# Filler products on TensorE through the routing of a two-choice expert tower

## What is computed

```python
h = embed_table[ids] @ proj_up.T                       # low-rank embedding, rank 64
h = h + attention(layernorm(h))                        # linear: no softmax, one sequence at a time
n = layernorm(h)
pg = softmax(n @ Wg + bg); gw, gi = top_k(pg, 2)       # 4 groups, two are taken
pe = softmax(n @ We + be); ew, ei = top_k(pe, 1)       # 4 experts in each group, one is taken
f(x) = gelu(x @ W1 + b1) @ W2 + b2                     # one expert, hidden size 768
out = sum of gw * ew * f_expert(n) over the two taken  # 16 experts in all
h = h + layernorm(out @ Wp + bp) * gamma + beta
```

## Time and profile before

| what | before |
|---|---|
| median of three runs | 295.75 us (295.14 to 296.15) |
| the profiled execution's own time | 294.89 us |
| its span | 293.1 us |
| mean granted clock of TensorE | 0.906 of full |
| TensorE matmul busy | 244.2 us (83%) |
| VectorE, ScalarE, GpSimd busy | 135.7, 113.3, 127.7 us |
| chain that ended last, by engine | PE 52%, DVE 16%, issue 15%, POOL 7%, ACT 5%, DMA 4% |

### The profile page before, as it was taken

How to read it: one execution, slowest core, us unless ns; L and a number is a source line. 1 busy time by engine, 2 the same in 40 slices (tenths; PEclk the granted TensorE clock), 3 DMA queues, 4 the chain that set the end, 5 groups by cost and what they waited for, 6 DMA issues and landing times.

```text
span 293.1 us, 8691 instructions
## 1 busy us (share of the span) xinstructions
PE 244.2 (83%) x3013; PEld 226.6 (77%) x3013; DVE 135.7 (46%) x498; ACT 113.3 (39%) x416; POOL 127.7 (44%) x142
## 2 busy tenths in 40 slices
PE   7899996210658999999999999999999999748960
PEld 7677774000558999999999999999999999747740
DVE  7616888879951324332233223322332332304795
ACT  4434557400002344244434433444344334408960
POOL 5773551447488445444544454445444441210000
PEclk9959999655577999999999999999999999969995
DMA  4410442060899995689729229595299220039022
GB/s 78 80 29 9 106 112 54 1 163 1 203 244 242 257 238 160 149 215 212 193 67 242 69 67 227 134 241 162 67 230 242 69 70 27 27 103 343 28 92 98
DMA packets 55034, 39.20 MB, mean 134 GB/s; under 512 B 30130, under 2 KB 52164, under 8 KB 55012
## 3 DMA queue, kind: packets, MB, share of 16 engines
q1 hardware_dynamic: 50004, 26.51, 38.1%
q0 software_dynamic: 5008, 12.43, 14.8%
HBM read 30.36 MB, written 8.55 MB: 133 GB/s over the span
## 4 chain that ended last, share of the span: by engine, by line
PE 52%; DVE 16%; issue 15%; POOL 7%; ACT 5%; DMA 4%; POOLq 0%; SPq 0%; DVEq 0%; ACTq 0%
PE pA L1213 20%; PE pY L1226 18%; POOL y_rows L513 3%; POOL xg L507 3%; PE pX L1200 2%; PE pA L1152 2%; PE pY L1136 2%; DVE ys L1005 2%; DMA xg<-x_rows,token_of 2%; DVE ys L900 2%; DVE ys L1010 2%; DMA ys<-y_rows 1%; PE pY L1137 1%; PE pY L1160 1%; PE pY L1080 1%
## 5 line engine op out<-in xcount | busy, mean ns | idle before, releaser
L652 ACT ACTIVATE hT<-pA,b_s 128x128 f32<-128x128 f32 x234 | 64.8, 375 | 115.5 <-PE pA L1213 115.5
L1213 PE MATMUL pA<-xs,W_s 64*128 64x128 f32 x1404 | 89.6, 278 | 0.9 <-DVE xs L956 0.9
L1213 PEld LDWEIGHTS pA<-xs,W_s 64*128 64x128 f32 x1404 | 84.4, 191 | 1.2 <-issue 1.2
L1226 PE MATMUL pY<-W_s,hT 64*128 64x192 f32 x936 | 83.7, 323 | 1.0 <-DVE yo L969 1.0
L1226 PEld LDWEIGHTS pY<-W_s,hT 64*128 64x128 f32 x936 | 76.3, 187 | 1.1 <-issue 1.1
L513 POOL DMA_INDIRECT y_rows<-yo,dest_of x39 | 38.6, 989 | 79.7 <-DVE yo L969 79.7
L967 DVE COPY yo<-pY 128x192 f32<-128x192 f32 x39 | 13.9, 358 | 108.2 <-PE pY L1226 108.2
L507 POOL DMA_INDIRECT xg<-x_rows,token_of x41 | 39.9, 974 | 15.5 <-issue 12.0
L956 DVE COPY xs<-pX 128x192 f32<-128x192 f32 x82 | 25.3, 350 | 10.1 <-PE pX L1200 7.1
L462 POOL TENSOR_SCALAR x<-h,mu,rs 128x192 f32<-128x192 f32 x16 | 16.7, 1049 | 21.3 <-DVEq L847 10.8
L1200 PEld LDWEIGHTS pX<-ident,xg 64*128 64x128 f32 x246 | 15.8, 138 | 3.7 <-issue 3.7
(11 more groups left out here) (243 smaller groups left out, 270.4 us busy)
## 6 DMA issues: line engine op xcount, KB each, us to landing
W_s<-in_L_ffn_W_dram SPq DMA_DIRECT2D x30, 288.0 KB, 5.2
W_s<-in_L_ffn_W_dram SPq DMA_DIRECT2D x15, 576.0 KB, 6.6
x_rows<-x SPq DMA_DIRECT2D x16, 192.0 KB, 2.7
ys<-y_rows SPq DMA_DIRECT2D x8, 384.0 KB, 6.2
out_dram<-ys SPq DMA_DIRECT2D x8, 192.0 KB, 1.9
xg<-x_rows,token_of POOLq DMA_INDIRECT x41
y_rows<-yo,dest_of POOLq DMA_INDIRECT x39
emb<-n_L_tok_embed_table_dram,ids POOLq DMA_INDIRECT x16, 2.5
```

Source lines behind the costliest of these rows:

```text
L652: ins = nc.scalar.activation(hT[v][:, j * P:(j + 1) * P], units(v, j), ACT.Gelu, bias=b1_s[u][:, j:j + 1])
L1213: mm = pe.matmul(units(v, n * HB + j), W1_s[u][rows, g, j * P:(j + 1) * P], xs[v][rows, g, :], start=(g == 0 and j == 0), stop=(g == DG - ...
L1226: mm = pe.matmul(pY[n][:, 0:D], hT[v][rows, j * P:(j + 1) * P], W2_s[u][rows, j, :], start=(j == 0), stop=(j == HC - 1))
```

## The change

`keep_busy` takes a count, is moved up, and is called at nine more places in the routing: 18 products ahead of the transposes of `b2_s`, 5 behind a new wait on `lg_exp`, 5 behind the counting products, 5, 6 and 6 behind new waits on `ends_known`, `runs_known` and `slots_known`, 4 behind the transpose of the experts' column, and 2 ahead of each group of eight one-hot products but the first. The group ahead of the first expert tile has 22 products in place of 9. The group ahead of the mixing keeps its 9. That is 55 calls in the routing and 13 more in the last group: 68 products, 136 passes.

```diff
@@ -1058,6 +1058,11 @@
             fill_idle(3, ident[:, :])
 
+            def keep_busy(count):
+
+                for _ in range(count):
+                    pe.matmul(pA[1][:, 0:P], ident[:, :], ident[:, :], start=True, stop=True)
+
             def turn_weights():
@@ -1162,32 +1167,39 @@
             pe.wait_ge(b2_in, 48)
             pe.wait_ge(h2_ev, B)
+            keep_busy(18)
             pe.transpose(ps_2m, b2_s[:, 0:P], ident[0:EX, 0:EX])
             pe.transpose(ps_2r, b2_s[:, P:D], ident[0:EX, 0:EX]).then_inc(b2T_mm, 1)
             pe.wait_ge(b2T_ev, 1)
             two(ps_2p, b2T_m[:, :], b2T_r[:, :], Wp_m[:, :], Wp_r[0:DR, :]).then_inc(b2p_mm, 1)
+            pe.wait_ge(lg_exp, 2)
+            keep_busy(5)
 
 
             pe.wait_ge(picked, 1)
             chosen = both[:, :, :].rearrange("p i e -> p (i e)")
             pe.matmul(ps_rank.rearrange("p i e -> p (i e)"), before[:, :], chosen, start=True, stop=True)
             pe.matmul(ps_tot, ones[:, :], both[:, :, :].rearrange("p i e -> p e i"), start=True, stop=True).then_inc(counted, 1)
+            keep_busy(5)
+            pe.wait_ge(ends_known, 1)
+            keep_busy(5)
+            pe.wait_ge(runs_known, 1)
+            keep_busy(6)
+            pe.wait_ge(slots_known, 1)
+            keep_busy(6)
             pe.wait_ge(b2p_ev, 1)
             pe.wait_ge(experts_counted, 1)
             pe.transpose(ps_expert_row, expert_f[:, :], ident[:, :]).then_inc(experts_mm, 1)
+            keep_busy(4)
             for m in range(K * NT):
+                if m and m % GROUP == 0:
+                    keep_busy(2)
                 pe.wait_ge(hot, (m // (GROUP // 2) + 1) * (GROUP // 2) if m >= 2 * GROUP else (m // GROUP + 1) * GROUP)
                 pe.wait_ge(hot_row, m // GROUP + 1)
                 mm = pe.matmul(ps_inv, hot_lane[:, m, :], hot_tile[:, m, :], start=(m == 0), stop=(m == K * NT - 1))
             mm.then_inc(inv_mm, 1)
 
-            def keep_busy(scratch):
-
-                for _ in range(BUSY):
-                    pe.matmul(scratch, ident[:, :], ident[:, :], start=True, stop=True)
-
-
-            keep_busy(pA[1][:, 0:P])
+            keep_busy(22)
@@ -1258,7 +1270,7 @@
             pe.wait_ge(moe_done, 1)
-            keep_busy(pA[1][:, 0:P])
+            keep_busy(BUSY)
```

## The result

The changed kernel takes 293.43 us (median of 20 runs, 291.15 to 299.28); the kernel before, timed in 20 runs, 295.14 us. The ratio is 0.9938 with a 95% interval of 0.991 to 0.9965: 0.35 to 0.9% faster, 1.0 to 2.7 us. The forecast was 293.7. A ratio here leaves out the runs that are over 1.5% above the fastest run of their kernel (four of the changed kernel's 20, none of the other's), so it can stand off the quotient of the medians.

A forecast was written before the change was run, and what follows sets the result against it. VectorE's chain was taken to bound the routing, TensorE everything from `turn(0)` on. Counting products 0, last one-hot products -0.2, `up(0)` -1.85, the rest covered: -2.05 us, from 295.75 to 293.7 us; range 292.7 to 295.6.

The forecast's parts named there:

- 1.85 us: First expert tile: gain expected from `up(0)` running at full clock, 2.06 us in place of 3.91.
- The clock lasts: Ahead of `up(0)`: with pauses of 1.5 and 0.9 us left, the clock stays full and `up(0)` takes 2.06 us.
- the first rival: The clock falls again ahead of `up(0)`, most of the gain goes: 295.0 to 295.6 us; chance 0.23.
- over its 3: Sign of being wrong, first tile: `up(0)` taking over 3 us in the profile after.
- under its 0.5: Sign of being wrong: TensorE waiting under 0.5 us for the gather ahead of `turn(0)`.
- End at 84.4, cover 1.5 us: Ahead of `turn(0)`: 22 products start at 79.4 at full clock, end at 84.4, 1.5 us before the gather; cost nothing.
- the second rival: Clock falls among the one-hot products, returns late; `turn(0)` 1.9 us late, sum about nothing: 295.8 us; chance 0.08.
- The one-hot products: VectorE's wait for the last ones in the routing: taken -0.2 us, bounds -0.3 and, at half clock, +0.9.
- Counting products: Routing: clock expected to fall before them, so no gain; bounds 0 and 0.3 us, taken 0.
- The other groups: Routing: 18 products and later fillers covered, cost nothing; clock falls once after 58.5, returns at 66.5 to 68.
- The third gather: Ahead of `turn(2)`, due at 90.2: gather there at about 90.0 or 89.8; if not, up to 0.5 us lost.
- The slower rival: 22 products at half clock take 10.3 us and delay `turn(0)`: +2.9 us, 298.6 us; chance 0.07.

The follow-up runs named there:

- P0: Probe pattern behind the changed kernel's output: no fillers in the routing, 9 products ahead of the first tile, as before; mean `up(0)` 4.04 us, ten draws.
- P1: Probe pattern behind the changed kernel's output: no fillers in the routing, 22 products ahead of the first tile; mean `up(0)` 2.28 us, ten draws.
- P3: Probe pattern behind the changed kernel's output: the routing's fillers and 22 products ahead of the first tile, as the change; mean `up(0)` 2.28 us, ten draws.
- the probes: Two runs of the changed kernel; behind its finished output TensorE repeats the routing's list and first tile, VectorE keeping time; no kernel time or ratio given.
- r1: The changed kernel measured again, unaltered: 293.50 us against 295.14 for the kernel before, ratio 0.9957.
- P5: Probe pattern: routing's fillers with 4 in place of 2 in each one-hot group, 22 products ahead of `turn(0)`, 3 behind; mean `up(0)` 2.54 us, ten draws.
- e2: The changed kernel with 9 products in place of 22 ahead of the first tile: 316.60 us against 316.58 for before, ratio 1.0039.
- e3: The changed kernel with 3 more products between `turn(0)` and `up(0)`: 315.80 us against 316.58 for before, ratio 1.0017.
- e7: The kernel before with 22 products ahead of the first tile, no fillers in the routing, measured again: 316.64 us against 316.70, ratio 0.9995.
- e5: The kernel before with 24 products ahead of `turn(0)` and 3 behind, no fillers in the routing: 316.30 us against 316.70, ratio 0.9994.
- e6: The kernel before with 32 products ahead of `turn(0)` and 3 behind, no fillers in the routing: 315.98 us against 316.70, ratio 0.9982.
- e1: The kernel before with 22 products in place of 9 ahead of the first tile, no fillers in the routing: 317.11 us against 316.58, ratio 1.0003.
- e4: The kernel before without its nine products ahead of `turn(0)`: 317.14 us against 316.58, ratio 1.0043.
- e8: The changed kernel with 25 products in place of 22 ahead of `turn(0)` and 3 behind: 315.17 us against 317.33 for before, ratio 0.9947.

## Why the prediction was right

**The 22 products and `up(0)`.** The mechanism holds: the 22 keep the clock in `up(0)`, as P0 against P1 and P3 shows. That it alone makes the gain is not shown (see Open). The size, 1.85 us, is a little too large. It is the chain's 3.91, which has the tail of `up(0)` in it, less its 2.06 for `up(1)`, which has none; like for like it is 3.91 less 2.28, 1.63 us, and up to 1.93 against the 4.21 of P0's slowest draws. Four of the five executions of the changed kernel have it (the two under the probes counted in). The step "The clock lasts" was right in those four; the fifth is the first rival, given 0.23. By the rule beside that rival (the Trainium skill, "TensorE: Matmul & The Clock Gate", Part 4: a transpose does not count as PE-busy for the gate in the way that a product does) the pause is one piece, and the gain goes. It did not go in those four, but there the piece was 1.4 to 1.9 us and not the 2.6 that the prediction priced. Whether transposes count, no run here shows.

The prediction named signs of being wrong, and some came. In the first profile `up(0)` took 3.80 us, over its 3. In three of the other four TensorE's wait for the gather was 0.1, 0.19 and 0.42 us, under its 0.5, and the clock lasted all the same: that sign had the wrong direction, since a short wait is what keeps the clock.

**Cover of the 22.** "End at 84.4, cover 1.5 us" was wrong. The clock falls among the one-hot products (at 76.7 after, between 73 and 74 in r1), which the prediction took for unlikely, and the 22 begin at half, the condition of the second rival (0.08). That rival had `turn(0)` 1.9 us late; but the 22 last 6.0 to 6.9 us and end 0.1 to 0.8 us ahead of the gather. The late group is what bridges the pause; at full clock, 5.2 us, it would have left a pause in which P5 lost the clock in two draws of four. So the number 22 was right by luck: an error in the step beneath it.

**The one-hot products.** -0.2 us was forecast; it is +0.15 (0.64 to 0.79 us). The two fillers among them at half clock cost what the bound of +0.9 had priced, though a sixth of it.

**Counting products.** Taken 0, bounds 0 to 0.3: VectorE's wait for them is 0.92 after, 0.84 in r1, where the clock fell only behind the start of the first (59.60, the fall at 59.8), and 0.93 before.

**The other groups.** The 18 products are covered, `b2T_m` is not late. The fall came, at 56.2 after, earlier than forecast and among the five behind `lg_exp`, and between 59 and 60 in r1; the return came by 66.5 in both. The Trainium skill ("TensorE: Matmul & The Clock Gate", Part 1) has the gate's moments not tied to the kernel's start. The traces agree as far as they go: counted from the first of the 18 products, the same code lost the clock after 7.1 us in one execution and after 12.1 in the other (r1).

**The third gather.** Priced at up to 0.5 us, which was too little. It was late in three of the five: with `up(0)` at 2.28 the way to `turn(2)` is 4.49 us when nothing waits (r1), and 5.14, 5.43 and 5.51 elsewhere, 0.65 to 1.0 us given back.

**The sum.** Forecast was a gain of 2.05 us, measured are 1.7 us between the medians of 20 runs each, with 1.0 to 2.7 for the interval. (The 293.7 starts from 295.75, the median of three runs, 0.6 us above that of the 20.) Over the five executions the way from `turn(0)` to `turn(2)` averages 5.34 us, 0.8 less than before's one execution and 1.4 less than the other one with nine products (e2). The probe's mean `up(0)` for before's nine, 4.04 us, lies between those two (3.91 and 4.21). With the 0.15 us of the routing taken off, 0.6 to 1.3 us. So the draws account for less than the forecast and for a part of the 1.7; only their upper end lies in the interval, and no row shows where the rest comes from.

**Faster by over 0.3%, 0.66:** it is. The slower rival (22 products at half to their end, 10.3 us) did not occur in any draw; the longest 22 took 7.2 us, those of the probes included.

**Open:** whether the routing's fillers do anything. By the clock the probe says no (P1 and P3 differ by 0.03 us), but its `turn(0)` waits for no gather. By time, none of the four kernels with 22 or more products and no fillers in the routing is clear of before (1.0003, 0.9994, 0.9982, 0.9995), and of the five measurements with both, four are (0.9938, 0.9957, 0.9954, 0.9947), e3 being the fifth. Within one group the change leads e7, e5 and e6 by 0.8, 0.5 and 0.2 us in the median, none of which is clear of the scatter. A difference would have to come by the gather. In the kernels the first gather took 7.0, 7.6 and 7.1 us without them (e1, e5, e7) but 5.3 and 5.4 as well (before, e4), and at most 6.5 in the eight with them. Five draws against eight don't settle whether that is chance. So the rival that both parts of the change are needed still stands.

## What to carry to other kernels

Where fillers are to hold TensorE's clock over the wait for a transfer, look at how much idle time they leave just ahead of the work they serve. Here 0.60 us or less kept the clock, and from 0.79 us on it was mostly lost. A group that was a little too long cost little: e8, with its fillers to the start of `turn(0)`, is level with the change. Size such a group by the clock at which it will begin, not by the one it is to bring about. And where a gain hangs on the clock, one profile of each kernel compares two draws; repeat the stretch in a probe, or profile the same kernel several times.

## What the runs showed that was not expected

The clock differs between executions of the same code far from any change: at half from 16 to 22.8 us in one, from 8.4 to 11.8 in another, not at all ahead of 50 us in a third (r1). The end of the attention moves with it, by 1.35 us (50.40 against 49.05) and again by 1.4 (47.64 in r1), each nearly as much as the change under test.

The first gather, at the same place in the program, took from 5.3 to 7.6 us from issue to `turn(0)` where TensorE waited for it. That decides how many fillers are enough: the 24 of e5 ended too soon for its 7.6.
